# GpSimd forms the low halves of queries and keys and adds the output's bias in a softmax attention

## The reference, cut to what matters

```python
xn = layernorm(x)
qkv = xn @ w_qkv + b_qkv
q, k, v = 16 heads of 8 channels each
attn = softmax(einsum('bhqd,bhkd->bhqk', q, k) * 8 ** -0.5)
s = einsum('bhqk,bhkd->bhqd', attn, v) @ w_proj + b_proj
x = x + s * silu(moe_0(xn))            # 8 experts, 2 per token
xn = layernorm(x)
x = x + linear_attention(xn) * silu(moe_1(xn))
```

## Time and profile before

| | |
|---|---|
| median of 3 runs | 1030.18 us (1027.87 to 1035.39) |
| the profiled execution, its own time | 1029.66 us |
| its span, first to last instruction | 1027.8 us |
| mean granted clock of TensorE, as a share of 2.4 GHz | 0.924 |
| busy: PE, DVE, ACT, POOL | 911.2, 823.9, 596.2, 550.5 us |
| attention's steps 1 to 32 | about 95 to 456 us of the span |

### The profile page before, as it was taken

One profiled execution on the slowest core, in us unless ns is written; L12 is line 12 of the kernel. 1 busy time (PEld: TensorE's weight loads), 2 busy tenths in 40 slices (PEclk: granted clock), 3 DMA queues, 4 the chain that ended last, 5 costly groups with the idle time before them and its releaser, 6 DMA issues.

```text
span 1027.8 us, 17766 instructions
## 1 busy us (share of the span) xinstructions
PE 911.2 (89%) x5384; PEld 590.5 (57%) x5384; DVE 823.9 (80%) x1875; ACT 596.2 (58%) x1234; POOL 550.5 (54%) x606
## 2 busy tenths in 40 slices
PE   4789999999999999989999954989996999999760
PEld 4544344443444344448888854746654888889760
DVE  7677999999999999615555548699995799999775
ACT  6216888888888888863333326323332777777552
POOL 7322388844444443004555536358785288887660
PEclk9559999999999999999999985699998999999895
DMA  6824656554535543035565744023412467776738
GB/s 200 309 80 146 204 178 214 160 170 131 182 114 177 167 149 104 16 116 192 190 209 179 235 142 123 20 85 110 126 58 88 158 220 219 206 222 212 236 114 250
DMA packets 120208, 164.79 MB, mean 160 GB/s; under 512 B 18321, under 2 KB 81906, under 8 KB 117042
## 3 DMA queue, kind: packets, MB, share of 16 engines
q1 hardware_dynamic: 94290, 109.08, 35.5%
q0 software_dynamic: 17376, 50.38, 14.0%
q10 hardware_dynamic: 8448, 4.20, 1.4%
HBM read 103.92 MB, written 60.06 MB: 160 GB/s over the span
## 4 chain that ended last, share of the span: by engine, by line
PE 50%; POOL 21%; issue 10%; DVE 9%; DMA 5%; ACT 3%; SPq 1%; ACTq 0%; POOLq 0%; DVEq 0%
PE ps L1174 12%; PE ps L1073 12%; POOL slots_x L842 8%; POOL token_y L892 8%; PE ps L1221 5%; PE ps L1079 5%; PE ps L366 3%; PE ps L368 3%; PE ps L367 3%; POOL stage L859 2%; DVE nmax L1735 2%; POOL everstd L866 2%; PE ps L1117 2%; PE ps L1163 1%; DMA stage<-token_y 1%
## 5 line engine op out<-in xcount | busy, mean ns | idle before, releaser
L1735 DVE TENSOR_REDUCE nmax<-ps 128x1 f32<-128x512 f32 x512 | 322.2, 681 | 32.2 <-PE ps L1079 30.9
L1346 ACT ACTIVATE stage<-ps 128x512 f32<-128x512 f32 x512 | 272.9, 594 | 60.9 <-PE ps L1073 56.9
L892 POOL DMA_INDIRECT token_y<-stage,ids_now x156 | 168.9, 1083 | 109.6 <-DVE stage L1794 52.2
L1079 PE MATMUL ps<-stage,stage 32*128 32x512 f32 x512 | 190.2, 507 | 10.8 <-DVE nmax L1735 9.2
L842 POOL DMA_INDIRECT slots_x<-xn,pos x128 | 153.5, 1199 | 40.8 <-issue 39.6
L1073 PE MATMUL ps<-stage,stage 32*128 32x512 f32 x512 | 166.4, 478 | 4.2 <-ACT stage L1346 3.6
L1073 PEld LDWEIGHTS ps<-stage,stage 32*128 32x128 f32 x512 | 66.8, 181 | 144.0 <-ACT stage L1346 126.9
L1174 PE MATMUL ps<-stage,stage 128*32 128x512 f32 x1024 | 136.4, 605 | 0.0
L1221 PE MATMUL ps<-stage,stage 128*128 128x128 f32 (+1 forms) x1092 | 132.2, 277 | 1.2 <-DVE stage L1864 1.0
L1221 PEld LDWEIGHTS ps<-stage,stage 128*128 128x128 f32 (+1 forms) x1092 | 127.6, 194 | 1.8 <-DVE stage L1864 1.4
L366 PE MATMUL ps<-stage,stage 128*128 128x512 f32 (+1 forms) x322 | 122.6, 381 | 4.1 <-ACT stage L1388 3.1
(11 more groups left out here) (244 smaller groups left out, 1492.5 us busy)
## 6 DMA issues: line engine op xcount, KB each, us to landing
stage<-halves_w SPq DMA_DIRECT2D x23, 1024.0 KB, 5.1
stage<-halves_w SPq DMA_DIRECT2D x23, 704.0 KB, 4.6
stage<-slots_x SPq DMA_DIRECT2D x32, 260.0 KB
stage<-q_halves SPq DMA_DIRECT2D x32, 256.0 KB
halves_w<-stage POOLq DMA_DIRECT2D x16, 512.0 KB, 3.2
k_halves<-stage SPq DMA_DIRECT2D x24, 256.0 KB
q_halves<-stage SPq DMA_DIRECT2D x24, 256.0 KB
stage<-k_halves SPq DMA_DIRECT2D x128, 48.0 KB
```

Of the source, the lines that this page charges most:

```text
L892: pool.indirect_dma_start(out=token_y, out_offset=bass.IndirectOffsetOnAxis(ap=ids_now[:, r, q:q + 1], axis=0), in_=ysb[:, r, q, :], in_of ...
L1079: pe.matmul(ps[:, (0, 1, 7)[bank_of(v, i)], :], head_rows(Qs, g2, j2)[:, t * P:(t + 1) * P], head_rows(Ks, g2, j2), start=True, stop=True) ...
L1346: act.activation(probs[:, t % 2, j, :], ps[:, 2 + bank_of(u, i), :], ACT.Exp, scale=SCALE).then_inc(exp_set, 1)
L1735: dve.tensor_reduce(nmax[:, g % 2, at:at + 1], ps[:, (0, 1, 7)[bank_of(v, i)], :], AX, ALU.max, negate=True).then_inc(max_set, 1)
```

## The change

The high half of sequences 2 to 7 is no longer written by ScalarE as `Hi`. ScalarE writes the projection with its bias in fp32 into `Lo`'s place; POOL copies it, rounded, into `Hi` and subtracts that in place. PE's waits for bank 6 go from `lo_set` to `hi_set` in steps from 0 on; SP's wait in `store_halves` stays with `lo_set`, which POOL now raises. POOL does this behind the weight piece of the step. The projected output is copied by ScalarE into `attn`, and POOL adds the bias there in steps with g = 1, the last two behind its scatters. VectorE has neither any more (sequences 0 and 1, ahead of step 0, stay as they were).

```diff
+            def split_half(b, o):
+                pool.wait_ge(hi_set, b * 2 + (o + 1))
+                x = Lo[:, 1 - o, :].bitcast(F32)
+                pool.tensor_copy(Hi[:, 1 - o, :], x).then_inc(pool_side, 1)
+                side[0] += 1
+                pool.wait_ge(pool_side, side[0])
+                pool.tensor_tensor(Lo[:, 1 - o, :], x, Hi[:, 1 - o, :].bitcast(F32), ALU.subtract).then_inc(lo_set, 1)
+            def add_output_bias(b):
+                pool.wait_ge(attn_set, b + 2)
+                pool.tensor_tensor(rows_of(attn, b), rows_of(attn, b), spread(bproj_bc[:, :], 1, [P, QT, D]),
+                                   ALU.add).then_inc(pool_side, 1)
+                side[0] += 1
...
                             if piece >= 5:
                                 pool.wait_ge(onorm_set, piece - 4)
                             split_piece(piece)
+                            u = piece - 4
+                            if u % GROUPS == 2 and 2 <= u < 24:
+                                split_half(u // GROUPS + 2, 0)
+                                split_half(u // GROUPS + 2, 1)
+                            if u % GROUPS == 1 and u > GROUPS:
+                                add_output_bias(u // GROUPS - 1)
+                if L == 0:
+                    add_output_bias(SEQS - 2)
+                    add_output_bias(SEQS - 1)
+                    pool.wait_ge(pool_side, side[0])
...
                         if now.halves:
-                            pe.wait_ge(lo_set, b * 2 + 6)
+                            pe.wait_ge(lo_set if u < 0 else hi_set, b * 2 + 6)
...
                         if now.next:
-                            pe.wait_ge(lo_set, b * 2 + 5)
+                            pe.wait_ge(lo_set if u < 0 else hi_set, b * 2 + 5)
                             project(0, b + 2, 6)
...
-                act.activation(Hi[:, 1 - o, :], ps[:, bank, :], ident_f, bias=cols[:, 1 - o:2 - o]).then_inc(hi_set, 1)
+                half = Hi[:, 1 - o, :] if b < 2 else Lo[:, 1 - o, :].bitcast(F32)
+                act.activation(half, ps[:, bank, :], ident_f, bias=cols[:, 1 - o:2 - o]).then_inc(hi_set, 1)
...
+                        if (t, j) == (3, 3) and g == 0 and now.tail:
+                            act.wait_ge(out_mm, b)
+                            act.activation(rows_of(attn, b - 1), ps[:, 6, :].rearrange("p (q d) -> p q d", q=QT),
+                                           copy_f).then_inc(attn_set, 1)
...
-                        if (t, j) == (0, 0) and now.halves:
+                        if (t, j) == (0, 0) and now.halves and u < 0:
                             low_half(b + 2, 1, 6)
-                        if (t, j) == (3, 0) and now.next:
+                        if (t, j) == (3, 0) and now.next and u < 0:
                             low_half(b + 2, 0, 6)
...
-                        if (t, j) == (3, 3) and g == 0 and now.tail:
-                            dve.wait_ge(out_mm, b)
-                            dve.tensor_tensor(rows_of(attn, b - 1), ps[:, 6, :].rearrange("p (q d) -> p q d", q=QT),
-                                              spread(bproj_bc[:, :], 1, [P, QT, D]), ALU.add).then_inc(attn_set, 1)
...
                     dve.wait_ge(silu_set[L], b + 1)
+                    if L == 0:
+                        dve.wait_ge(pool_side, 2 * (SEQS - 2) + SEQS)
```

More of the change, by code:

```diff
@@ L313, in build @@
         rden_set = sem("rden_set")
+        pool_side = sem("pool_side")
         vT_mm, vT_set, vtp_mm, vaug_set = sem("vT_mm"), sem("vT_set"), sem("vtp_mm"), sem("vaug_set")
@@ L800, in split_piece @@
                                raw_halves[:, r, :, 0:F].bitcast(F32)).then_inc(halves_stored[r], 16)
+            side = [0]
+            def split_half(b, o):
[10 more added lines that the diff above has]
+                side[0] += 1
             def outer(m):
```

## The result

The kernel after takes 1067.26 us (median of 4 runs, 1063.72 to 1079.84), the one before 1030.76 us in its 4 runs: ratio 1.0338, interval 1.0282 to 1.0393. The run of 1079.84 us lies 1.5% above the fastest and is left out of the ratio. The profiled execution of after takes 1065.29 us, 35.6 us more than that of before (1029.66 us); its span is 1063.5 us, 35.7 us more.

What follows compares the result with a forecast made beforehand. Attention taken as bound by PE, DVE close behind, with POOL's in-order list deciding. Stall 36.4, clock +3, later halves -4, bias 0 sum to +35.4 us on 1029.66 us: 1065 us, range 1050 to 1090 us.

Steps and rivals of the forecast that it cites:

- The stall: Ahead of step 5: SP's store waits for POOL's late sequence 2 halves, delaying PE +36.4 us (34 to 38.5).
- The landing: End of the stall: step 5's row maximum lands 2.9 us after issue, bounds 0.58 to 5 us.
- The clock: Behind the stall: PE restarts at granted 0.50, rises some 5 us later; +3 us, between 2 and 10.
- The later halves: Sequences 3 to 7: POOL is level, DVE's low halves no longer delay PE; -4 us, bounds 0 to -12.
- The bias: Output's bias: ScalarE's copy costs 0.4 us against DVE's 0.69 us saved; 0, at worst +3 us.
- DVE: VectorE's busy time: down 8 to 9 us for twelve halves and 5.5 us for eight adds.
- DVE beside a busier POOL: Attention stretches: DVE is not slowed when POOL is busier, so nothing is charged.
- The sum: Whole kernel: +35.4 us on the profiled execution's 1029.66 us, giving 1065 us.
- A: Rival: after the stall PE's clock stays low, up to 10.3 us a step; 1103 us for four steps; chance 0.12.
- B: Rival: no stall at sequence 2, only gains left; 1025 us (1016 to 1030); chance 0.06.
- C: Rival: SP also waits in steps 7, 11, 15, 19 and 23, 4 us each; 1085 us; chance 0.04.

Runs made afterwards that it cites:

- e1_front2: Against the changed kernel, sequence 2's halves moved ahead of the first scatter in POOL's list; 1047.21 us in one run.
- e4_piece3: Against the changed kernel, sequence 2's halves put behind weight piece 3 instead of piece 6 in POOL's list; 1042.08 us in one run.
- e6_store_later: Against the changed kernel, SP stores sequence 2's halves one step later, POOL's list the same; 1058.83 us in one run.
- e5_clock: Changed kernel plus 32 dense matmuls on PE ahead of step 5, once both sequence 2 halves are written; 1059.88 us, ratio to before 1.0293.
- e9_by_clock_again: e2_by_clock with its line numbers shifted by three and no other edit; 1026.63 us, ratio to before 0.9987.
- e7_bias_only: Against the changed kernel, halves stay on VectorE as before, only the output's bias goes to ScalarE and POOL; 1030.57 us in one run.
- e2_by_clock: Changed kernel with sequence 2's halves ahead of the first scatter, sequence 3's behind piece 6, sequence 4's behind piece 13; 1027.77 us, ratio to before 0.9968.

## Why the prediction was right, step by step

**The stall** (step 5's first matmul predicted 36.4 us later than before, measured 172.63 - 138.54 = 34.1; the gap itself is 35.4, because PE's wait began 1.3 us earlier, by the early start and by sequence 2's gain, swallowed as foreseen). The mechanism came as described, and e1_front2, e4_piece3 and e6_store_later show that it is the place in POOL's list and SP's order. Three terms of the sum were mis-sized. POOL's first scatter started 1.6 us earlier in this execution (115.77 against 117.33 us), so the halves were written at 160.4 and 162.3 us, not at 162.1 and 164.1 (-1.7); this start varies between executions, from 114.92 us (e4_piece3) to 118.47 us (e6_store_later) among kernels with the same list ahead of it. The sum counts from the first half's end although its text has the store wait for both halves. The sum was right: in `store_halves` the key stores wait for the first half alone, and they went out 0.03 us behind it. From there to the issue of m_lo it took 8.15 us, not 9.9 (-1.7). The query stores took 1.99 us where I had carried over 2.83, but more of it is a wait that I carried over without seeing it. In before this row stands ahead of the row maximum:

```profile
129.03 0.35 SPq L506 DMA_DIRECT2D stage<-q_halves  x1
```

It ends at 129.38 us and the row maximum goes out at 130.84 us: 1.46 us in which SP waited for the maximum. In after the same two rows stand 0.11 us apart, since the maximum had long been ready. The landing took 4.06 us (172.63 - 168.57), not 2.9, within its bounds (+1.2).

**The clock** (predicted +3, measured +4.6, by e5_clock). Here the basis was wrong: I took the 5 us until the clock rises from a row of dense matmuls. e5_clock confirms that row for such matmuls (5.7 us from 163.49 us), but behind the attention's own mixture of 32-row scores and outputs it was back only after 12.1 us in after, 12.5 us in e1_front2, 13.8 us in e6_store_later and 8.7 us in e4_piece3. The loss was 4.6, 4.8, 4.9 and 3.2 us, less than half of each stretch (worked out from the row maxima as for after; in e1_front2 22.12 at n = 11 less -2.83 at n = 8 less the gap; in e6_store_later 32.85 at n = 8 less 1.38 at n = 5 less the gap, with sequence 3's 0.73 us put back). The upper bound of 10 us covered it.

**The later halves** (predicted -4, measured -3.6, five times 0.73 us). I took 0.41 us for each half. Both low halves of a sequence lie in one interval of the table (in before those at 206.00 and 209.06 us, between the row maxima at 200.18 and 212.45 us), so its 0.73 us are the gain of both, and 0.82 us was close. The split can be read in e9_by_clock_again, whose row maximum is 3.45 us ahead of before's at the start of this interval and 4.19 us at its end. The scores that waited for a maximum in the earlier trace rows, here before first, then e9_by_clock_again,

```profile
208.59 0.49 PE L1079 MATMUL ps<-stage,stage 32*128 32x512 f32 x1
```

```profile
204.69 0.39 PE L1115 MATMUL ps<-stage,stage 32*128 32x512 f32 x1
```

are 3.90 us ahead: about 0.45 us are won by there, as the prediction read from that wait, and about 0.3 us come with the second half.

**The bias** (predicted 0, measured -0.9 in after, -1.0 in e7_bias_only). I had ScalarE's copy push the next exponentials 0.4 us back. In e9_by_clock_again the copy ahead of step 5 begins at 136.15 us and the exponentials at 136.65 us; that execution runs 2.50 us ahead of before, where they begin at 139.13 us. So the copy puts the exponentials back by 0.02 us, not by 0.4, and what DVE no longer does shows as a small gain.

**DVE** was to lose 14.4 us of busy time; its low halves fell from 11.8 to 2.9 us and its adds from 5.5 us to nothing, as forecast, and the engine's total fell by 12.9 us. **DVE beside a busier POOL** was charged with nothing, and the rows of e2_by_clock agree (43.04 us in both stretches). The Trainium skill, GPSIMD Engine Reference, section Key points, has GpSimd and VectorE contend for SBUF interfaces when VectorE has two SBUF inputs or a two-port mode; no run here shows that cost, for maxima that read PSUM.

**The sum.** 1065 us predicted for the profiled execution, 1065.29 us measured. Against the predicted terms the stall gave -2.3, the clock +1.6, the halves +0.4 and the bias -0.9; the hand-over (+1.1) and the rest of the kernel (+0.6) stood in no term. The steps were right in kind and each within its bounds, the stall only just (34.1 of 34 to 38.5); that they meet to 0.3 us is luck.

**The rivals.** A, a clock that stays low, did not come: both later stretches of after show 1.00. Its doubt was right in part, though: behind the attention's matmuls the clock was back after 12.1 us, behind the dense ones of e5_clock after 5.7 us. B, no stall, did not come; e2_by_clock shows that it would have come with other places in the list, and that its price, 4.8 us, was fair for the attention (5.4 us won there, the bias included). C, a stall each sequence, did not come in after. e1_front2 shows how near it was: a second stall is there as soon as the first doesn't bring POOL level.

**What stays open.** The version placed by the clock is no measurable gain. Its attention is 5.3 to 5.4 us shorter in every trace, half a per cent, while the four whole-kernel comparisons of its kind read 0.9968, 0.9983, 0.9987 and 0.9987, each with an interval that takes in 1. The time from the table load to the end varies from 569.5 to 574.8 us between the profiles, without an order that follows the edits. Whether part of the gain is given back there can't be told from these runs.

## What to carry to other kernels

Before work is moved to an engine that looks idle, read at what time that engine's list reaches the place where the work is put; a busy share of 54% hid that POOL was 40 us behind the attention there and waited for it only later. Then follow who waits for the result and what is queued behind the waiter: here a store that nobody needed soon held up the small transfer that the next step needed. And price a pause of TensorE as its length plus the clock behind it, with the recovery taken from the same kind of matmuls that run there, as far as a row shows it.

## What the runs showed of the hardware that was not expected

After a pause of more than 18 us the granted clock came back from 0.50 to 1.00 after 5.7 us under dense 128-row matmuls (one run), but only after 8.7 to 13.8 us under the attention's mixture (four runs), although PE is shown as busy for practically all of both (5.50 of 5.50 us in e5_clock; 7.37 of 7.40 us and 4.00 of 4.00 us in after). At the hand-over to the experts the granted clock was 1.00 in some executions and 0.50 to 0.59 in others, even of one program.
